# Residual block of two 3x3 convolutions: second weights transposed between the phases, unread transposes ahead of each phase, alpha loaded by ScalarE's queue

## The reference: what is computed

```python
def lsq_quantize(w, alpha):      # Qn = -4, Qp = 3
    alpha_s = alpha * g + stop_gradient(alpha - alpha * g)
    wc = jnp.clip(w / alpha_s, Qn, Qp)
    return (wc + stop_gradient(jnp.round(wc) - wc)) * alpha_s
def batchnorm(x, gamma, beta):
    mean, var = x.mean((0, 2, 3)), x.var((0, 2, 3))
    return gamma * (x - mean) * rsqrt(var + BN_EPS) + beta
out = conv3x3(x, lsq_quantize(w1, alpha1))
out = relu(batchnorm(out, gamma1, beta1))
out = conv3x3(out, lsq_quantize(w2, alpha2))
out = batchnorm(out, gamma2, beta2)
return relu(out + x)
```

## Time and profile before

| | us |
|---|---|
| median of 3 runs | 1489.55 (1488.96 to 1489.67) |
| the profiled execution | 1491.95, its span 1490.0 |
| TensorE (PE) busy | 1136.8, 76% |
| VectorE (DVE) busy | 1141.8, 77% |
| ScalarE (ACT) busy | 855.4, 57% |
| GpSimd (POOL) busy | 306.3, 21% |
| DMA | 297.00 MB, 199 GB/s over the span |

### The profile page before, as it was taken

How to read it: one execution, slowest core, us unless ns; L and a number is a source line. 1 busy time by engine, 2 the same in 40 slices (tenths; PEclk the granted TensorE clock), 3 DMA queues, 4 the chain that set the end, 5 groups by cost and what they waited for, 6 DMA issues and landing times.

```text
span 1490.0 us, 18697 instructions
## 1 busy us (share of the span) xinstructions
PE 1136.8 (76%) x5802; PEld 1033.1 (69%) x5802; DVE 1141.8 (77%) x1626; ACT 855.4 (57%) x1263; POOL 306.3 (21%) x147
## 2 busy tenths in 40 slices
PE   5999998999999999699999999999999400000000
PEld 5999987999999998699999999999999400000000
DVE  7999996788888886898888888888888632322324
ACT  3555555555556565677777777777777532222224
POOL 3333221122222222322222222222222100000000
PEclk9999999999999999899999999999999855555555
DMA  3455443455542220022244455554230699999999
GB/s 162 168 189 196 184 173 118 152 196 187 198 186 86 86 86 0 1 87 87 86 172 172 172 194 194 192 196 170 89 129 5 246 428 430 430 430 430 429 429 408
DMA packets 28110, 297.00 MB, mean 199 GB/s; under 512 B 3888, under 2 KB 3888, under 8 KB 4912
## 3 DMA queue, kind: packets, MB, share of 16 engines
q1 hardware_dynamic: 22608, 245.25, 41.7%
q10 hardware_dynamic: 5472, 51.38, 8.1%
HBM read 174.59 MB, written 122.03 MB: 199 GB/s over the span
## 4 chain that ended last, share of the span: by engine, by line
issue 64%; DMA 18%; POOL 14%; DVE 1%; ACT 1%; POOLq 1%; ACTq 0%; DVEq 0%
POOL v_lo L422 14%; DMA slots<-conv_spill 10%; DMA out<-slots 4%; DMA xbuf<-in_x 3%; DVE slots L872 1%; ACT slots L619 1%; POOLq L427 0%; POOLq L421 0%; POOLq L77 0%; POOLq L422 0%; ACTq L623 0%; DVE affine L793 0%; DVE tiny L790 0%; DVE affine L792 0%; POOL ident L408 0%
## 5 line engine op out<-in xcount | busy, mean ns | idle before, releaser
L422 POOL TENSOR_TENSOR v_lo<-v_rows,v_hi 128x1008 fp32r<-128x1008 f32 x128 | 304.0, 2395 | 835.1 <-ACT v_hi L474 835.1
L925 PE MATMUL conv_psum<-d_hi,w1T 128*128 128x398 f32 (+2 forms) x864 | 289.0, 338 | 11.0 <-ACT w2T L440 8.1
L925 PE MATMUL conv_psum<-d_hi,w2T 128*128 128x398 f32 (+2 forms) x864 | 285.8, 335 | 12.4 <-DVE d_lo L691 12.4
L925 PE MATMUL conv_psum<-d_lo,w1T 128*128 128x398 f32 (+2 forms) x864 | 286.6, 336 | 0.0
L925 PE MATMUL conv_psum<-d_lo,w2T 128*128 128x398 f32 (+2 forms) x864 | 284.1, 333 | 0.0
L512 ACT ACTIVATE squares<-slots,minus_shift 128x1008 bf16 (+3 forms) x192 | 225.0, 1172 | 13.7 <-ACT squares L512 8.9
L905 PE MATMUL conv_psum<-v_lo,w1T 128*128 128x512 f32 x576 | 227.1, 394 | 0.0
L905 PE MATMUL conv_psum<-v_lo,w2T 128*128 128x512 f32 x576 | 227.0, 394 | 0.0
L905 PE MATMUL conv_psum<-v_hi,w2T 128*128 128x512 f32 x576 | 226.8, 394 | 0.3 <-POOL v_lo L422 0.2
L905 PE MATMUL conv_psum<-v_hi,w1T 128*128 128x512 f32 x576 | 226.8, 394 | 0.0
L619 ACT ACTIVATE slots<-slots,affine 128x3136 f32<-128x3136 f32 (+1 forms) x34 | 93.6, 2754 | 209.1 <-DVE slots L872 208.3
(11 more groups left out here) (79 smaller groups left out, 1511.3 us busy)
## 6 DMA issues: line engine op xcount, KB each, us to landing
conv_spill<-slots SPq DMA_DIRECT2D x44, 1568.0 KB, 6.1
slots<-conv_spill SPq DMA_DIRECT2D x44, 1568.0 KB, 10.8
slots<-in_x SPq DMA_DIRECT2D x31, 1568.0 KB, 8.9
out<-slots ACTq DMA_DIRECT2D x30, 1568.0 KB, 11.7
xbuf<-in_x SPq DMA_DIRECT2D x28, 1568.0 KB, 52.0
xbuf_w<-in_x SPq DMA_DIRECT2D x4, 1568.0 KB, 51.6
out<-slots ACTq DMA_DIRECT2D x4, 784.0 KB, 10.5
slots<-in_L_conv_w SPq DMA_DIRECT2D x2, 576.0 KB, 9.7
```

The source lines that it names most:

```text
L422: nc.gpsimd.tensor_tensor(pair_window(1, k), pair_rows(k), pair_window(0, k).bitcast(F32), ALU.subtract).then_inc(pool_lo_ready, 1)
L925: last = nc.tensor.matmul(bank_run(CHUNK_BANK[j], r1 - r0), w[:, kh * 3 + kw, :], run(d_plane[half], r0 - WINO + 1, r1 - WINO + 1, kw - 1) ...
```

## The change

- The three lots of second weights are transposed after phase 1's last product (`second_weights`), into banks 6, 7 and 0, and ScalarE copies them after its last squares of phase 1. The lots in images 10 to 12 are gone. On TensorE and ScalarE the loop over pairs of images starts at image 2; VectorE's starts at image 10.
- `keep_busy(7, 56)` issues 56 transposes of the identity into bank 7, which nobody reads: in phase 1 once the first weights have landed, in phase 2 once the affine constants are ready.
- alpha1 and alpha2 are loaded at the head of ScalarE's queue and not at the head of SP's.
- In the last step of a phase, `add_totals` of the image before comes behind the rows of the last image.
- At the end of phase 2 the waits for the y2 stores come earlier; residual loads 3, 4 and 5 wait for the last chunk and product, and load 6 for the last sum. The w2T memory becomes buffer 5, and the sixth arena buffer becomes number 6.

```diff
@@ -107,7 +107,7 @@
                    for k, part in enumerate(("hi", "lo"))]
         m1, m3, d1, s1 = (placed(name, N, F32, TEMPS + k * N) for k, name in enumerate(("m1", "m3", "d1", "s1")))
         xbuf = [placed(f"xbuf{b}", PIX, F32, b * PIX)[:, :] for b in range(ARENA_XBUFS)]
-        xbuf.append(nc.alloc_sbuf_tensor_at("xbuf_w2", [C, PIX], F32, offset=w2_base)[:, :])
+        xbuf.insert(5, nc.alloc_sbuf_tensor_at("xbuf_w2", [C, PIX], F32, offset=w2_base)[:, :])
         ident = sb("ident", [C, C], BF16)
         alpha_in = sb("alpha_in", [C, 2], F32)
         gb = sb("gamma_beta", [C, 4], F32)
@@ -233,9 +233,8 @@
 
 
         W_LOTS = [[(0, 8), (8, 9), (9, 17), (17, SUMS)], [(0, 8), (8, 16), (16, SUMS)]]
-        W_BANK = [[0, 1, 2, 3], [7, 7, 7]]
-        W2_FIRST = 10
-        EXPLICIT = 14
+        W_BANK = [[0, 1, 2, 3], [6, 7, 0]]
+        EXPLICIT = 10
         TAKES = 6
 
         def w_bank(k, h):
@@ -285,9 +284,6 @@
             def squared_through(g):
                 sp.wait_ge(squared, g * NSQ + NSQ)
 
-            for k, a in enumerate((alpha1, alpha2)):
-                sp.dma_start(alpha_in[:, k:k + 1], a.rearrange("(a n) -> a n", a=1).to_broadcast([C, 1])
-                             ).then_inc(alpha_landed, 16)
             sp.dma_start(w_raw[0], w1.rearrange("o c a b -> o (c a b)")).then_inc(w_landed[0], 16)
 
             top = (WINO - 1) * W
@@ -374,20 +370,16 @@
             sp.wait_ge(lo_ready, STEPS * LO)
             sp.wait_ge(pool_lo_ready, STEPS * PLO)
             load_residual(2)
+            for b in range(2):
+                sp.wait_ge(y2_stored[b], 16 * (SPILL // 2))
 
             sp.wait_ge(chunk_done, STEPS * NC)
-            sp.wait_ge(sums_ready, STEPS * SR)
-            load_residual(5)
-
             sp.wait_ge(m_done, STEPS * M)
             load_residual(3)
             load_residual(4)
-            for b in range(2):
-                sp.wait_ge(y2_stored[b], 16 * (SPILL // 2))
-
-
-            sp.wait_ge(m_done, STEPS * M)
-            sp.wait_ge(chunk_done, STEPS * NC)
+            load_residual(5)
+
+            sp.wait_ge(sums_ready, STEPS * SR)
             load_residual(6)
 
             for j in range(IMAGES):
@@ -432,6 +424,9 @@
 
         @block.scalar
         def _(act):
+            for k, a in enumerate((alpha1, alpha2)):
+                act.dma_start(alpha_in[:, k:k + 1], a.rearrange("(a n) -> a n", a=1).to_broadcast([C, 1])
+                              ).then_inc(alpha_landed, 16)
             for k, v in enumerate((gamma1, beta1, gamma2, beta2)):
                 act.dma_start(gb[:, k:k + 1], v.rearrange("(c n) -> c n", n=1)).then_inc(small_landed, 16)
 
@@ -518,8 +513,7 @@
                 nc.scalar.activation(y, y, ACT.Relu, bias=affine[:, 0, 1:2],
                                      scale=affine[:, 0, 0:1]).then_inc(relu_ready, 1)
 
-            def step(g, p, b, phase, first=False, second=False, last=False, input_ready=None, relu_next=None,
-                     w2_lot=None):
+            def step(g, p, b, phase, first=False, second=False, last=False, input_ready=None, relu_next=None):
                 if not last:
                     input_ready()
                     hi_direct(g + 1, p + 1)
@@ -535,8 +529,6 @@
                     square(g - 1, p + (SLOTS - 1), 1 - b, phase, 2)
                 if not last:
                     hi_pairs(g + 1)
-                if w2_lot is not None:
-                    take_w2(w2_lot)
                 if relu_next is not None:
                     relu_next()
                 if not last:
@@ -563,14 +555,14 @@
                 take_chunk(0, 0, 0, j)
             phase1(0, 0, 0, first=True)
             phase1(1, 1, 0, second=True)
-            for n in range(2, EXPLICIT):
-                phase1(n, n % 2, n // 2, w2_lot=n - W2_FIRST if n in range(W2_FIRST, W2_FIRST + 3) else None)
-            with act.Fori(EXPLICIT // 2, (IMAGES - 2) // 2) as i:
+            with act.Fori(1, (IMAGES - 2) // 2) as i:
                 for b in range(2):
                     phase1(i * 2 + b, b, i)
             phase1(IMAGES - 2, 0, (IMAGES - 2) // 2)
             step(IMAGES - 1, IMAGES - 1, 1, 0, last=True)
             finish_phase(IMAGES - 1, IMAGES - 1, 1, 0)
+            for h in range(3):
+                take_w2(h)
 
 
             def phase2(m, b, first=False, second=False, last=False, landed=None):
@@ -755,12 +747,14 @@
                     make_v(g + 1)
                 first_difference(g)
                 second_difference(g)
-                if not first:
+                if not first and input_ready is not None:
                     add_totals(g - 1, 1 - b, phase)
                 if input_ready is not None:
                     lo_of_pair(g + 1, 0)
                 second_sum(g)
                 rows_out(g, p, b)
+                if input_ready is None:
+                    add_totals(g - 1, 1 - b, phase)
                 if first:
                     find_shift(g, phase)
 
@@ -943,29 +937,36 @@
                 if j == NC - 1:
                     pe.wait_ge(wT_ready, TAKES)
 
-            def lot_of_w2(n):
-                def transposes(j):
-                    if j == NC - 1:
-                        pe.wait_ge(w_int_ready[1], 2)
-                        pe.wait_ge(evac_done, n * NC + 2)
-                        transpose_lot(1, n - W2_FIRST)
-                return transposes
+            def second_weights():
+
+                pe.wait_ge(w_int_ready[1], 2)
+                pe.wait_ge(evac_done, IMAGES * NC)
+                pe.wait_ge(m_copied, IMAGES * 2 - 1)
+                for h in range(3):
+                    transpose_lot(1, h)
+                pe.wait_ge(wT_ready, 2 * TAKES)
+                pe.wait_ge(affine_ready, 1)
+                keep_busy(7, 56)
+
+            def keep_busy(bank, n):
+
+                for _ in range(n):
+                    nc.tensor.transpose(psum[:, bank, :].bitcast(BF16)[:, 0:C], ident[:, :], ident[:, :])
 
             pe.wait_ge(ident_ready, 1)
+            pe.wait_ge(w_landed[0], 16)
+            keep_busy(7, 56)
             pe.wait_ge(w_int_ready[0], 1)
             transpose_lot(0, 0)
             transpose_lot(0, 1)
             pe.wait_ge(wT_ready, 2)
             pe.wait_ge(pads_ready, PADS)
             convolve(0, wT[0], rest_of_w1)
-            for n in range(1, EXPLICIT):
-                if n in range(W2_FIRST + 1, W2_FIRST + 4):
-
-                    pe.wait_ge(wT_ready, TAKES + (2, 5, TAKES)[n - 1 - W2_FIRST])
-                convolve(n, wT[0], lot_of_w2(n) if n in range(W2_FIRST, W2_FIRST + 3) else None)
-            with pe.Fori(EXPLICIT // 2, IMAGES // 2) as i:
+            convolve(1, wT[0])
+            with pe.Fori(1, IMAGES // 2) as i:
                 for b in range(2):
                     convolve(i * 2 + b, wT[0])
+            second_weights()
             convolve(IMAGES, wT[1])
             convolve(IMAGES + 1, wT[1])
             with pe.Fori(IMAGES // 2 + 1, IMAGES) as i:
```

## The result

The changed kernel took 1476.76 us, the median of 4 runs (1475.88 to 1479.68), against 1489.61 us before (1488.96 to 1489.82); ratio 0.9918, 95% interval 0.9901 to 0.9935. That is 12.85 us less, where 16.5 had been forecast, and 1476.76 lies above the forecast range (1470.9 to 1475.3). The profiled execution took 1477.26 us, with a span of 1475.2; before it was 1491.95 and 1490.0.

The account below looks back on a forecast made before the run. TensorE bounds both phases and DMA the last stage. 14.7 + 0.95 + 0.35 - 1.5 + 0 + 2.05 = 16.5 us takes the median from 1489.55 to 1473.0 us; range 1470.9 to 1475.3.

Parts of the forecast that it names:

- part 1: Images 10 to 13 of phase 1: moving the second weights between the phases removes 14.69 us, copies covered; gain 14.7.
- part 2: Last step of phase 1: totals behind the rows bring the affine constants 0.95 us earlier; gain 0.95, not counted in phase 2.
- part 3: Start of phase 1: weights issued 0.9 us earlier, alpha landing at the same time; gain 0.35 us (0.5 lost to 0.42 gained).
- part 4: Chunks 0 to 2 of phase 1: clock raised early, then lost behind a longer wait for the bank; 1.5 us lost.
- forecast pause of 3.7 us: TensorE's wait before the first chunk 2 of phase 1, growing from 1.72 to 3.7 us, then 0.50 clock.
- part 5: Start of phase 2: faster chunks 0 and 1 win 1.6 us, but the third product waits for GpSimd's v_lo; 0.
- rival (c): Phase 2: an earlier d_hi closes VectorE's gap before d_lo, so GpSimd's first v_lo waits, 1.4 us: 1474.4; chance 0.05.
- part 6: Last stage: SP's residual loads start 2.1 us sooner and the end follows; gain 2.05 us (0.95 to 2.2).
- Rival (a): Both phase starts: unread transposes do not raise the clock; sum 15.7, time 1473.85 us; chance 0.33.
- Rival (b): Phase 1: the clock is raised and survives the pause; gain 18.0 us, time 1471.5; chance 0.09.
- Rival (d): Phase 1 loops of TensorE and ScalarE: six more passes stall at branches; 2.2 us a pass would leave 1486; chance 0.03.
- rival (e): Copies or moved waits do nothing as meant; the end gains only 0.95 us from earlier constants: 1474.1; chance 0.05.

Follow-up runs that it names:

- the second profile: The kernel before, unchanged, profiled once more: span 1487.4 us; its 10 executions took 1489.43 to 1494.19 us, median 1492.01.
- its own experiment: The kernel before with only the second weights' transposes moved between the phases, no unread transposes: 1477.51 us against 1490.25, ratio 0.9913.
- two variants: The changed kernel with gamma and beta at the head of SP's queue, 1476.18 us; the changed kernel without phase 1's unread transposes, 1478.13 us.

## Why the prediction was wrong

Two terms failed, by about the same amount, and the others nearly cancel. Alpha was taken as 0.35 gained and lost 2.05. The second weights were taken off the median as 14.7 and were worth 11.9 to 12.7 there. With the measured terms the sum is 12.7 + 0.94 - 2.05 - 0.7 + 0 + 1.9 = 12.8, against 12.85 measured; that this fits so closely is partly luck, since 12.7 comes from other executions and the 0.7 is known to 0.3 or so.

**Second weights (part 1).** Right in the profile: 14.66 us against 14.7, copies covered, no cost of the loops. Wrong as a step to the median. The prediction subtracted the profiled execution's saving from a median that lay 2.4 us below that execution. But the 2.4 us were in the removed steps themselves: the profiled execution had the clock fall behind all three pauses, and the second profile, of an execution at 1489.43, behind one. There the part is worth 11.9; in the medians of its own experiment it is 12.7. That is 2.0 to 2.8 us less than forecast.

**Totals (part 2).** Right: 0.94 us at the phases' boundary. The prediction let it count once; alone on the kernel before it counts twice, since the loads' last wait is for a sum. In the changed kernel the run of loads no longer waits for it, only the last load does.

**Alpha (part 3).** The step whose mechanism failed. It was taken as 0.35 gained, with a bound of 0.5 lost, because alpha is issued as early on one queue as on the other. The time of issue was right and the landing was not: 5.7 and 7.6 us instead of 3.6 and 5.2, because the weights' packets now run beside alpha's. The weights' first operation came 2.05 us later. In the medians alpha's place costs 1.9 us. No row stood behind the bound of 0.5. The kernel before had one to look at: the four small loads of gamma and beta on ScalarE's queue, issued from 0.74 to 2.15 with the weights issued at 1.66, took 3.7 to 7.8 us to land.

**Unread transposes ahead of phase 1 (part 4).** Right in its mechanism, as shown by the kernel with alpha on SP: pause of 2.92 us, clock at 0.50, first product 1.6 us late. In the changed kernel it came out another way, with alpha late. The 56 transposes ran at the low spacing (6.03 us). The nine behind them took 0.68 us instead of 1.12, so the clock had risen by then. Behind the pauses of 1.99 and 1.23 us it fell again, and chunk 0 ran slowly throughout (windows view of the kernel after):

```profile
16.40:22.40 6.00, 6.00 (x18) 5.73 (x18) 5.86 (x8) 0.27 (x1) 0.00 (x0) 0.50 0.37 151
```

So the second group of w1T copies came at 23.13 and held back the casts by some 0.6 us. The term was 1.5 lost in the forecast and about 0.7 in the profile (0.4 to 1.0 by the two profiles without the transposes). The forecast pause of 3.7 us was 1.40 here.

**Unread transposes ahead of phase 2 (part 5) and rival (c).** The value of 0 was right for the profiled execution, and for the reason given, GpSimd's v_lo. The clock rose 4.4 us after the first of them and not 3.3, so the 56 took 5.39 us and not 4.9. Rival (c) had the right place and cause, but a chance of 0.05 and a price of 1.4. It costs about 3.2 us, since GpSimd gets no turn behind d_lo either and the clock falls behind TensorE's wait. By their times it was met by 1 of 4 executions of the changed kernel, 1 of 4 and 2 of 4 of two variants, and 0 of 4 of the one with alpha on SP; of these only one was profiled. The changed kernel's execution of 1479.68 is put down to it by its time. The Trainium skill, "SBUF — State Buffer", section "SBUF: two separate sides", says that a VectorE operation with two SBUF inputs and a GpSimd operation that reads SBUF lock each other out for the whole instruction, and that whichever starts first gets the ports. The trace agrees that they exclude each other: GpSimd's v_lo took 8.65 us and ended 2.0 us after VectorE's row of operations, about the 2.1 us that it takes alone. It does not agree on the order: in that profile the v_lo had begun at 601.99, before q_rows (602.79) and p_rows (604.95), and still came behind them.

**Residual loads (part 6).** 1.9 us in the profile, 2.5 to 2.7 alone, against 2.05.

**Rival (a)** fell, though the sign named for it, a spacing of 0.11 us throughout, was there in phase 1: the granted clock rose while nothing but unread transposes ran. Windows view of the kernel after, over the 56 of phase 2:

```profile
591.40:595.70 4.30, 4.26 (x41) 4.29 (x42) 1.38 (x1) 4.27 (x3) 0.00 (x0) 0.50 0.02 4
596.00:596.60 0.60, 0.60 (x14) 0.60 (x12) 0.60 (x1) 0.60 (x1) 0.00 (x0) 1.00 0.00 0
```

The rule of the Trainium skill, "TensorE: Matmul & The Clock Gate", Part 4, that the transpose mode does not engage the full clock, does not hold for these. **Rival (b)** fell with the pauses behind which the clock did not survive. **Rival (d)** fell too, with all steps at 17.57, as did **rival (e)**, since the copies and the moved waits did what was meant.

## What to carry to other kernels

Before a saving read from one profiled execution is taken off a median, find where that execution differs from the median: if it is in the part that is removed, the difference must not be counted twice. A tiny load on the critical path needs its head start over the large ones, and another queue issued at the same time does not give it. TensorE became faster ahead of a wait and gained nothing in phase 2 and lost in phase 1; it also closed a gap in VectorE's work that GpSimd lived on. So look behind the next wait before buying speed ahead of it.

## What the runs showed of the hardware

- Two loads of 0.5 KB landed 2.1 and 2.4 us later beside a load of 576 KB that was issued with them than ahead of it.
- After a pause of TensorE of 2.3 to 2.8 us the clock fell in one execution and not in another of the same program; after pauses of 2.9 to 3.1 it fell in each profile, and after 1.7 or less where TensorE had been at work steadily before it did not.
- A pause of 1.99 us, nine transposes and a pause of 1.23 us let it fall in the kernel after, soon after it had been raised (0.50 from 16.40 to 22.40).
- A GpSimd tensor operation of 2.1 us took 8.65 us while VectorE issued operations with two SBUF inputs without a gap, in two kernels alike.
- At the start of the kernel after, the granted clock's column reads 1.00 while 56 transposes take 6.03 us, 0.11 us each. That is the pace of those that ran at 0.50 in phase 2 (41 in 4.30 us), so the column is of use only from its first change on.
